# Router weights built inside the layernorm loop, two matmul groups instead of three per recurrence step, three input buffers instead of four

## The reference

```python
xn = layernorm(x)                                  # x: [2, 8192, 1024]
u, sp = xn @ Wi.T, xn @ Ws.T                       # [.., 128]
state = tanh(state @ A.T + u_t @ B.T) + sp_t       # for every t, state: 128 values
ys = states @ C.T;  attn = ys @ Wo.T
logits = xn @ router_weight                        # 8 experts
w = softmax of the top 2 logits, zero elsewhere
gate, up = xn @ Wg[e], xn @ Wu[e]                  # 1024 -> 1024 each, all 8 experts
act = (clip(up) + 1) * min(gate, 7) * sigmoid(1.702 * gate)
ffn = sum over e of w[:, e] * (act @ Wd[e])
return x + attn + ffn
```

## Time and profile before

| what | us |
|---|---|
| median of 2 runs | 1694.83 (1694.64 to 1695.03) |
| the profiled execution: time | 1694.75 |
| its span on the slowest core (core 0) | 1693.2 |
| spans of the other cores | 1689.1 to 1691.6 |
| span to the end of the column loop | about 136 |
| router weights | about 136 to 157 |
| recurrence | about 158 to 351, fill until about 309 |
| attention output | about 351 to 391 |
| expert 0's down projection and experts 1 to 7 | 391 to 1693 |

### The profile page before, as it was taken

One profiled execution on the slowest core, in us unless ns is written; L12 is line 12 of the kernel. 1 busy time (PEld: TensorE's weight loads), 2 busy tenths in 40 slices (PEclk: granted clock), 3 DMA queues, 4 the chain that ended last, 5 costly groups with the idle time before them and its releaser, 6 DMA issues.

```text
span 1693.2 us, 25899 instructions; the slowest of 8 cores (1689.1 to 1693.2 us)
## 1 busy us (share of the span) xinstructions
PE 1490.1 (88%) x6998; PEld 670.4 (40%) x6998; DVE 902.1 (53%) x2133; ACT 559.8 (33%) x1013; POOL 120.9 (7%) x230
## 2 busy tenths in 40 slices
PE   0444888479999999999999999999999999999984
PEld 0221444213444444444444444444444444444432
DVE  3554777232466536653665366536653665366543
ACT  3432222351255115511552155215521552155200
POOL 2000000000000000000000000000000000000011
PEclk9756999658999999999999999999999999999995
DMA  6400112001122212222222222222222222222058
GB/s 143 108 26 1 26 29 35 13 1 21 31 38 39 44 31 38 39 44 32 39 38 44 32 38 39 44 32 38 38 43 33 36 40 38 38 38 39 14 110 214
DMA packets 36314, 74.66 MB, mean 44 GB/s; under 512 B 4864, under 2 KB 4864, under 8 KB 36176
## 3 DMA queue, kind: packets, MB, share of 16 engines
q0 software_dynamic: 31424, 55.71, 21.6%
q1 hardware_dynamic: 4752, 17.30, 3.0%
HBM read 120.10 MB, written 8.39 MB: 76 GB/s over the span
## 4 chain that ended last, share of the span: by engine, by line
PE 82%; DMA 5%; DVE 5%; ACT 4%; issue 3%; DVEq 0%; ACTq 0%; POOL 0%; POOLq 0%; SPq 0%
PE pb L287 26%; PE pb L867 25%; PE pb L277 25%; DMA xres<-xm 2%; PE pb L681 1%; PE pb L737 1%; PE pb L742 1%; DVE etu L313 1%; ACT G L703 1%; PE pb L479 1%; ACT et L326 1%; DMA y<-otm 1%; PE pb L694 1%; DVE acc L883 1%; PE pb L491 1%
## 5 line engine op out<-in xcount | busy, mean ns | idle before, releaser
L277 PE MATMUL pb<-xn_fm,wgu 128*128 128x512 bf16 x2048 | 495.1, 383 | 1.2 <-ACT wbc L656 1.0
L287 PE MATMUL pb<-xn_fm,wgu 128*128 128x512 bf16 x2048 | 489.1, 380 | 0.0
L867 PE MATMUL pb<-act_w,wdb_ 128*128 128x512 bf16 x2048 | 450.7, 382 | 6.8 <-DVE acc L883 5.9
L883 DVE TENSOR_TENSOR acc<-acc,pb 128x512 bf16<-128x512 bf16 x256 | 176.0, 687 | 276.9 <-PE pb L867 274.3
L867 PEld LDWEIGHTS pb<-act_w,wdb_ 128*128 128x128 bf16 x2048 | 201.2, 99 | 253.8 <-issue 17.9
L277 PEld LDWEIGHTS pb<-xn_fm,wgu 128*128 128x128 bf16 x2048 | 198.8, 99 | 241.0 <-issue 11.8
L287 PEld LDWEIGHTS pb<-xn_fm,wgu 128*128 128x128 bf16 x2048 | 198.3, 98 | 234.8 <-issue 3.7
L307 ACT CAST etu<-pb 128x512 bf16<-128x512 f32 x224 | 131.1, 585 | 255.6 <-PE pb L287 255.6
L326 ACT ACTIVATE et<-etg 128x512 bf16<-128x512 bf16 x256 | 161.2, 630 | 96.3 <-DVE etg L318 62.1
L305 ACT CAST etg<-pb 128x512 bf16<-128x512 f32 x224 | 131.1, 585 | 91.6 <-PE pb L277 90.7
L321 DVE TENSOR_SCALAR etu<-etu,sbu 128x512 bf16<-128x512 bf16 x256 | 91.8, 359 | 110.5 <-ACT etu L307 104.9
(11 more groups left out here) (105 smaller groups left out, 514.1 us busy)
## 6 DMA issues: line engine op xcount, KB each, us to landing
wgu<-Wg POOLq DMA_DIRECT2D x64, 256.0 KB, 3.5
wgu<-Wu POOLq DMA_DIRECT2D x64, 256.0 KB, 3.5
wdb_<-Wd POOLq DMA_DIRECT2D x64, 256.0 KB, 3.5
xln<-xm SPq DMA_DIRECT2D x16, 512.0 KB, 4.1
y<-otm SPq DMA_DIRECT2D x16, 512.0 KB, 5.5
xres<-xm POOLq DMA_DIRECT2D x16, 256.0 KB, 5.9
xln<-xw SPq DMA_DIRECT2D x1, 512.0 KB, 4.8
sWiT<-WiT POOLq DMA_DIRECT2D x1, 256.0 KB, 5.6
```

The costliest lines, as they stand in the source:

```text
L277: e.matmul(bg_[:, 0:STW], wgu[:, 2 * par, dc, :], rhs, start=(dc == 0), stop=(dc == NDC - 1)),
L287: e.matmul(bu2[:, 0:STW], wgu[:, 2 * par + 1, dc, :], rhs, start=(dc == 0), stop=(dc == NDC - 1)),
L867: e.matmul(bk[:, 0:STW], wdb_[:, par, ic, :], act_w[:, ic, stt * STW:(stt + 1) * STW], start=(ic == 0), stop=(ic == NDC - 1), skip_group_c ...
L883: e.tensor_add(acc[:, fc, stt * STW:(stt + 1) * STW], acc[:, fc, stt * STW:(stt + 1) * STW], bk[:, 0:STW]),
```

## The change

Three edits. `xln` has 3 buffers instead of 4, so a load waits for the tile three before it. The router weights are no longer built after the column loop: `emit_tail4(g)`, the same work for token tiles 4g to 4g+3 and their L650 and L656, is emitted at the end of columns 18 to 21; its transposes all go through PSUM bank 5, each waiting for the copy of the one before, and the sigmoid is taken in two parts, for tiles 0 to 11 in column 18 and 12 to 15 in column 21. `pump(6)` ahead of the recurrence goes, and a step pumps 2 units instead of 3: 128 x 2 = 256.

```diff
-        xln = _es.enter_context(nc.sbuf_tensor("xln", [128, 4, DM], F32))
+        xln = _es.enter_context(nc.sbuf_tensor("xln", [128, 3, DM], F32))
...
-                    if tc >= 4:
-                        pv, ps = ln_free[par4]
+                    if tc >= 3:
+                        pv, ps = ln_free[par3]
                         wl = [("s_ve", pv), ("s_sc", ps)]
...
+                def sig_batch(bi, lo, hi):
+                    s_sig = sc(lambda e, lo=lo, hi=hi:
+                               e.activation(rsg[:, 1, lo:hi], rsg[:, 0, lo:hi],
+                                            ACT.Sigmoid),
+                               wait=[("s_ve", cnt["s_ve"])])
...
+                def emit_tail4(g):
+                    if g == 0:
+                        sig_batch(0, 0, 12)
+                    if g == 3:
+                        sig_batch(1, 12, 16)
+                    for mc in range(4 * g, 4 * g + 4):
...
+                        t6w = [("s_ve", wt_done[rpar])]
+                        if mc >= 1:
+                            t6w.append(("s_sc", router_evac[(mc - 1) % 2]))
+                        t6 = te(lambda e, wt=wt:
+                                e.transpose(pb[5][0:8, 0:128], wt, sI32[:]),
+                                wait=t6w)
...
                         if 5 <= col < NMC + 5:
                             emitR1(col - 5)
+                        if 18 <= col <= 21:
+                            emit_tail4(col - 18)
...
-                for mc in range(NMC):
-                    rpar = mc % 2
...
-                    tbank = pb[5 - rpar]
...
-                pump(6)
                 for s in range(NSTEP):
-                    pump(3)
+                    pump(2)
```

More of the change, by code:

```diff
@@ L377, in emitLoad @@
                 def emitLoad(tc):
-                    par4 = tc % 4
+                    par3 = tc % 3
                     wl = []
-                    if tc >= 4:
-                        pv, ps = ln_free[par4]
+                    if tc >= 3:
+                        pv, ps = ln_free[par3]
                         wl = [("s_ve", pv), ("s_sc", ps)]
                     lxsem = "s_lx%d" % (tc % 2)
-                    lxv = dma("sy", lxsem, xln[:, par4], x_srcs[tc], wait=wl)
+                    lxv = dma("sy", lxsem, xln[:, par3], x_srcs[tc], wait=wl)
                     lnA[tc] = (lxsem, lxv)
@@ L388, in emitA @@
                     par = tc % 2
+                    par3 = tc % 3
                     lxsem, lxv = lnA[tc]
-                    xl = xln[:, tc % 4]
+                    xl = xln[:, par3]
                     ssum = stat[:, par * 8 + 0: par * 8 + 1]
@@ L411, in emitB @@
                     par = tc % 2
-                    xl = xln[:, tc % 4]
-                    xn = xnb[:, tc % 3]
+                    par3 = tc % 3
+                    xl = xln[:, par3]
+                    xn = xnb[:, par3]
                     negm = stat[:, par * 8 + 1: par * 8 + 2]
@@ L431, in emitB @@
                     if tc >= 3:
-                        xwl.append(("s_te", xnb_free[tc % 3]))
+                        xwl.append(("s_te", xnb_free[par3]))
                     v4 = ve(lambda e, xn=xn, xl=xl, negm=negm, inv=inv:
@@ L436, in emitB @@
                     inv_free[par] = cnt["s_sc"]
-                    ln_free[tc % 4] = (v4, s2)
+                    ln_free[par3] = (v4, s2)
                     lnB[tc] = v4
@@ L574, in emitR2 @@
                                     e.tensor_sub(d12, m1, m2))
+                wt_done = {}
+                bc0_ev = {}
+                v_dfs = {}
+                def sig_batch(bi, lo, hi):
[3 more added lines that the diff above has]
+                               wait=[("s_ve", cnt["s_ve"])])
+                    ve(lambda e, lo=lo, hi=hi:
+                       e.tensor_scalar(rsg[:, 2, lo:hi], rsg[:, 1, lo:hi],
+                                       -1.0, 1.0, ALU.mult, ALU.add),
+                       wait=[("s_sc", s_sig)])
+                    v_dfs[bi] = ve(lambda e, lo=lo, hi=hi:
+                                   e.tensor_scalar(rsg[:, 3, lo:hi], rsg[:, 1, lo:hi],
+                                                   2.0, -1.0, ALU.mult, ALU.add))
@@ new lines, in emit_tail4 @@
+                def emit_tail4(g):
[4 more added lines that the diff above has]
+                    for mc in range(4 * g, 4 * g + 4):
+                        rpar = mc % 2
+                        wt = wtm[:, rpar]
+                        tmp8 = rt[:, rpar, 5:13]
+                        vwl = []
+                        if mc < 2:
+                            vwl.append(("s_ve", v_dfs[0]))
+                        elif mc in (12, 13):
+                            vwl.append(("s_ve", v_dfs[1]))
+                        if mc >= 2:
+                            vwl.append(("s_te", r_t6[rpar]))
+                        ve(lambda e, wt=wt, mc=mc:
+                           e.tensor_scalar(wt, eq2b[:, mc, :], rsg[:, 2, mc:mc + 1],
+                                           None, ALU.mult), wait=vwl)
+                        ve(lambda e, tmp8=tmp8, mc=mc:
+                           e.tensor_scalar(tmp8, eqmb[:, mc, :], rsg[:, 3, mc:mc + 1],
+                                           None, ALU.mult))
+                        wt_done[rpar] = ve(lambda e, wt=wt, tmp8=tmp8:
+                                           e.tensor_add(wt, wt, tmp8))
+                        t6w = [("s_ve", wt_done[rpar])]
[4 more added lines that the diff above has]
+                                wait=t6w)
+                        r_t6[rpar] = t6
+                        router_evac[rpar] = sc(
+                            lambda e, mc=mc:
+                            e.copy(w_fmb[0:8, mc * 128:(mc + 1) * 128],
+                                   pb[5][0:8, 0:128]),
+                            wait=[("s_te", t6)])
+                    stt = g
+                    bwl = [("s_sc", cnt["s_sc"])]
+                    if stt == 0:
+                        bwl.extend(lc_wait)
+                    else:
+                        bwl.append(("s_sc", bc0_ev[stt - 1]))
+                    m_ = te(lambda e, stt=stt:
+                            e.matmul(pb[3][:, 0:STW], ssel[:, 0:128],
+                                     w_fmb[:, stt * STW:(stt + 1) * STW],
+                                     start=True, stop=True),
+                            wait=bwl)
+                    bc0_ev[stt] = sc(
+                        lambda e, stt=stt:
+                        e.copy(wbc[:, 0, stt * STW:(stt + 1) * STW],
+                               pb[3][:, 0:STW]),
+                        wait=[("s_te", m_)])
```

## The result

| | median of its runs, us | ratio to before, 95% interval |
|---|---|---|
| before | 1694.64 | 1 |
| changed | 1676.93 | 0.989 (0.9877 to 0.9904) |

The kernel is 1.1% faster. 1674 us was forecast, in a range of 1658 to 1686. The profiled execution took 1675.5 us with a span of 1674.0 on core 0.

A forecast was written before the change was run, and what follows sets the result against it. PE is always busy from the down projection on, so its start decides: 31.9 us won in the recurrence, 11.0 lost ahead of it, 20.9 us earlier. 1694.75 - 20.9 = 1673.9, forecast 1674 us, range 1658 to 1686.

The forecast's parts named there:

- The down projection's start: End of the attention output, after which PE is always busy: starts 20.9 us earlier than 391.14 us.
- The attention output and its clock: Stage after the recurrence: same 39.8 us, clock fallen again to 1.2 GHz (0.50) after PE waits about 4 us.
- rival 2: Clock stays up through the attention output: at most 12.5 us less, 1661.5 us; chance 0.08.
- The period: Recurrence, one fill tile per four steps: 4.83 us per tile, 5.05 for 8 tiles in the last 32 steps.
- Rivals 1 and 3: Recurrence's tile period: 1, DVE's 4.31 us, total 1656 us, chance 0.07; 3, 5.5 us, total 1695 us, chance 0.10.
- The router's move: Columns 18 to 21: moved work delays what is queued behind it, first fill matmul at 168.8 against 157.75, 11.0 us lost.
- The single PSUM bank: Router groups' transposes: one bank costs nothing, 0.85 us per transpose under DVE's 1.02; otherwise below 8 us.
- Rival 5: Router's work at the column loop's end fits in PE's and DVE's gaps: 11 us less, 1663 us; chance 0.06.
- Three buffers: Input loads in the column loop: each waits for the L434 three tiles back, at no cost.
- Ends 0 and +2, I take 0: Cost of three input buffers: between 0 and 2 us, taken as 0.
- the constants' wait: PE's 20.86 us wait until 41.16 us covers late first loads; without it some 2 us would be lost.
- The sign that the prediction named for it: Column loop: an L395 released by a DMA beyond 41 us would show the forecast wrong.

The follow-up runs named there:

- e4: Kernel before without pump(6), two units a step, each tile's sigmoid and two multiplications emitted after that step's tanh: 1649.93 us, ratio 0.9737.
- e1: Changed kernel with the old fill put back, pump(6) and three units a step: 1707.35 us, ratio 1.0074.
- e3: Kernel before with three input buffers (`xln`) instead of four, nothing else: 1697.23 us, ratio 1.0014.
- e8: e4 with the up half's PSUM copy on ACT and the last 32 tanh written side by side, the add reading strided: 1641.5 us, ratio 0.9688.
- e6: e4 without the 32 8-row matmuls adding the down projection's bias in the attention output: no ratio, shortest execution 1646.3 us.

## Why the prediction was right, and where it wasn't

- **The place.** The down projection's start decided: forecast 20.9 us earlier, measured 20.7 on the slowest cores, 19.8 as the mean of 8. The attention output and its clock (0.50) were as put: the clock fell in the 4 us in which PE waited for L728 (on core 0 it was 1.00 until 328.5 and 0.50 from 330.5 on). So rival 2 fell. By the rule of the Trainium skill (TensorE: Matmul & The Clock Gate, "The HAM clock gate") the clock would have come up in this stage; PE was busy 94% of it (36.68 of 39 us) and the clock did not rise.
- **The period.** 4.83 us forecast, 4.82 measured in most tiles; 5.05 forecast for the last 8, 5.14 measured (from the sigmoid at 287.31 to 328.41). Five tiles before took up to 0.4 longer. From the first fill to the add that gives 162.9 us against 161.7 forecast, so 1.2 us of the gain did not come. Holding back the sigmoid (e4) took the stall away, so this was its cause, shown and not only argued. Rivals 1 and 3 did not happen: no period of 4.31 in the changed kernel, and none of 5.5.
- **The router's move.** 11.0 us forecast, 10.3 measured (e1 against e3, by the trace). On core 0, counted from the end of tile 12's top two, it is 167.64 - 120.35 = 47.3 us to the first fill against 157.75 - 121.42 = 36.3 before: 11.0. That it is so exact is partly luck, since two steps inside were off and cancelled. From the last transposes to `emit_usp(3)` 3.25 was taken, and it was 130.78 - 128.40 = 2.4: before, ACT's copy of the tile stood behind a small copy that waited for DVE. From `emit_usp(4)` to the end of the next top two the 4.5 of before were taken, and it was 5.4: the granted clock was 0.50 there (147.7 to 150.9), after 9 us in which PE had only the group's small matmuls, and 1.00 before (129.8 to 132.2), so that 8 matmuls of 128 columns took 1.01 us instead of 0.61. The single PSUM bank cost nothing, as put. Rival 5 fell with e1.
- **Three buffers, the step that failed.** "Ends 0 and +2, I take 0" rested on the 7.5 us between L434 and the L395 that reads the buffer next, with the constants' wait as cover for the first loads. The first loads were covered. The steady ones were late, for the other reader: ACT's L406 comes 4 to 5 us before L395. Its margin was 2.1 us for a load that took 3.5. The term was 2.4 us by the ratio (0.7 to 4.2), 2.6 by the trace, just outside its range. The sign that the prediction named for it, an L395 released by a DMA, could not have shown it.
- **What was luck.** The lost 2.6 us of the buffers and 1.2 of the recurrence should have put the down projection some 3 us later than forecast. They did not, because the constants, a term that the sum does not have, arrived at 38.74 us instead of 41.16 on core 0 (mean of 8 cores 39.0 instead of 41.2). Whether that belongs to the three buffers or to the execution is not shown. The time fell by 18.6 us by the ratio, 2.3 less than forecast.

## What to carry to other kernels

Follow one chain through the lists of in-order engines with the durations of the trace: an instruction that waits holds everything behind it, so emit it after the latency-bound step and not before (here 14 to 16 us for an order alone). Spread filling work evenly along a latency-bound chain, and then count each engine's time per unit of fill, for the next bound is there. Where a buffer is taken away, look for its earliest reader on any engine. Work that is moved into a loop to hide it can just as well delay the loop.

## What was not expected of the hardware

- A tanh of 128x64 values writing bf16 with a stride of 64 bytes takes 0.45 us, against 0.22 side by side (e8). An add of 128x512 bf16 values that reads one of its sources with a stride of 128 bytes takes 1.02 us (e8), against 0.43 without.
- The granted clock stayed at 0.50 through 39 us of PE work at 94% busy, and also with full 128-row matmuls alone at 70% busy (e6), while at the recurrence's start it was 1.00 within 6 us of the first fill matmul (167.64; 0.54 from 170 to 173, 1.00 from 173 on), PE being busy nearly all of that time.
